# Normalising the residual: row sums with its formation, squares on ScalarE, scale and bias in one operation

## Time and profile before

| | before |
|---|---|
| median of 3 runs | 555.94 us (555.14 to 557.07) |
| the profiled execution | 554.49 us, its span 552.7 us |
| PE matmul busy | 446.5 us (81%) |
| DVE busy | 438.0 us (79%) |
| ACT busy | 376.4 us (68%) |
| POOL busy | 262.7 us (48%) |
| chain that ended last | PE 45%, DVE 25%, ACT 13%, issue 6%, DMA 6% |
| `stats` of `r` (L763), 32 instructions | 408 to 430 ns each |
| scaling of `r` (L664), 32 instructions | 583 to 601 ns each |
| L1168, 8 instructions | 1209 to 1231 ns each |

### The profile page before, as it was taken

One profiled execution on the slowest core, in us unless ns is written; L12 is line 12 of the kernel. 1 busy time (PEld: TensorE's weight loads), 2 busy tenths in 40 slices (PEclk: granted clock), 3 DMA queues, 4 the chain that ended last, 5 costly groups with the idle time before them and its releaser, 6 DMA issues.

```text
span 552.7 us, 11601 instructions
## 1 busy us (share of the span) xinstructions
PE 446.5 (81%) x2730; PEld 385.8 (70%) x2730; DVE 438.0 (79%) x1423; ACT 376.4 (68%) x928; POOL 262.7 (48%) x194
## 2 busy tenths in 40 slices
PE   0196899967999996587978999999999999999200
PEld 0045888856888885446867897999999999999200
DVE  6999795999898988775887776877777777777185
ACT  5992864455667565884656676777777777777266
POOL 0000359545467877375155534444354444445446
PEclk9998999999999996897989999999999999999755
DMA  6302830032223574398146465545454467645495
GB/s 153 154 1 71 336 127 1 0 133 78 100 92 133 175 231 159 122 337 280 40 109 144 82 121 139 82 79 79 71 85 79 78 110 157 119 78 68 85 376 228
DMA packets 48190, 70.34 MB, mean 127 GB/s; under 512 B 7680, under 2 KB 37248, under 8 KB 47744
## 3 DMA queue, kind: packets, MB, share of 16 engines
q1 hardware_dynamic: 34832, 51.82, 29.1%
q0 software_dynamic: 13296, 17.80, 19.3%
HBM read 37.90 MB, written 31.70 MB: 126 GB/s over the span
## 4 chain that ended last, share of the span: by engine, by line
PE 45%; DVE 25%; ACT 13%; issue 6%; DMA 6%; SPq 2%; POOL 2%; DVEq 1%; ACTq 0%; another core or an unknown queue 0%; POOLq 0%
PE psum L1518 15%; PE psum L1542 13%; PE psum L1528 4%; DMA y_rows<-yw,row_of 3%; PE psum L1438 3%; PE psum L1502 2%; ACT acc L735 2%; DVE ws L958 2%; DVE st L763 2%; PE psum L1396 2%; ACT dump L674 2%; PE psum L1458 2%; DVE o L1170 1%; ACT ws L611 1%; PE psum L1409 1%
## 5 line engine op out<-in xcount | busy, mean ns | idle before, releaser
L1343 POOL DMA_INDIRECT y_rows<-yw,row_of x71 | 110.6, 1558 | 140.3 <-SPq L405 74.7
L1518 PE MATMUL psum<-ws,z_hl 128*128 x426 | 119.3, 416 | 12.6 <-DVE ws L958 5.6
L1542 PE MATMUL psum<-ws,h_hl 128*128 x852 | 116.5, 286 | 0.6 <-DVE h_hl L1124 0.6
L1542 PEld LDWEIGHTS psum<-ws,h_hl 128*128 128x128 f32 x852 | 104.1, 189 | 0.8 <-issue 0.8
L1518 PEld LDWEIGHTS psum<-ws,z_hl 128*128 128x128 f32 x426 | 76.2, 192 | 28.0 <-issue 14.9
L1299 POOL DMA_INDIRECT z_rows<-zn,pos x64 | 70.4, 1099 | 26.2 <-issue 17.6
L656 ACT ACTIVATE hg<-hb 128x512 f32<-128x512 f32 x71 | 44.9, 632 | 31.7 <-DVE hb L1118 26.0
L1438 PE MATMUL psum<-yf,it 128*128 128x256 f32 x256 | 60.8, 394 | 2.6 <-DVE r L1144 2.6
L619 ACT ACTIVATE z_f<-psum,gb 128x128 f32<-128x128 f32 x142 | 57.1, 452 | 6.6 <-PE psum L1502 2.7
L1409 PE MATMUL psum<-pm,ft 128*128 128x256 f32 x256 | 58.2, 382 | 0.4 <-DVE tmp L944 0.4
L649 ACT CAST h_hl<-psum 128x512 fp32r<-128x512 f32 x71 | 41.5, 585 | 24.9 <-PE psum L1528 23.2
(11 more groups left out here) (223 smaller groups left out, 826.0 us busy)
## 6 DMA issues: line engine op xcount, KB each, us to landing
z_in<-z_rows SPq DMA_DIRECT2D x71, 129.5 KB
w_raw<-in_dram SPq DMA_DIRECT2D x16, 512.0 KB, 5.7
xs<-in_dram SPq DMA_DIRECT2D x8, 512.0 KB, 5.5
x_dram<-xs SPq DMA_DIRECT2D x8, 512.0 KB
y_rows<-zn SPq DMA_DIRECT2D x8, 512.0 KB, 3.3
yr<-y_rows SPq DMA_DIRECT2D x8, 512.0 KB, 7.4
out_dram<-acc SPq DMA_DIRECT2D x6, 512.0 KB, 2.7
b1r<-in_dram SPq DMA_DIRECT2D x8, 256.0 KB
```

Of the source, the lines that this page charges most:

```text
L1343: pool.indirect_dma_start(y_rows, bass.IndirectOffsetOnAxis(ap=row_of[:, t:t + 1], axis=0), yw[t % 6][:, :], None, compute_op=ALU.add).the ...
L1518: last = TE.matmul(ps_h[q], z_hl[q][:, a, k], w_at(e, c, k * F, F), start=n == 0, stop=n == 5)
L1542: last = TE.matmul(ps_y[q], h_hl[q][:, a, k], w_at(e, c, 1024 + k * H, H), start=n == 0, stop=n == 11)
```

## The change

- The two instructions that form `r` become four of 256 columns, each with its row sum (`accum_out`). `bn_stats` and `bn_aggr` of `r` go. One small operation makes the negative mean and signals `r_mean`.
- ScalarE, in place of normalising `r`, squares `r` with the mean as bias and sums the squares into `mv[2]`, signals `var2`, and takes the root with the scale 1/H.
- VectorE computes `(r - mean) * ln_w` in four instructions, after `scales_x1` and `find` and before `point` (in the last step before all of them).
- The reciprocal of the deviation moves behind `place`; L1168 goes; the four instructions that added `ln_b` now multiply by the reciprocal too.

```diff
@@ sigma (ScalarE)
-                                     scale=(1.0, 1.0 / H, 1.0, (1.0 + EPS) / H)[slot]).then_inc(sem(f"sd{slot}"), 1)
+                                     scale=(1.0, 1.0 / H, 1.0 / H, (1.0 + EPS) / H)[slot]).then_inc(sem(f"sd{slot}"), 1)
@@ step (ScalarE)
                 if cur.live:
+                    act.wait_ge(sem("r_mean"), cur.b + 1)
+                    for k in range(4):
+                        last = nc.scalar.activation(dump[:, k], r[:, k], ACT.Square, bias=mv[2][:, k, 0:1],
+                                                    accum_out=mv[2][:, k, 1:2])
+                    last.then_inc(sem("var2"), 1)
                     sigma(cur, 2)
-                    act.wait_ge(sem("st_r"), cur.b + 1)
-                    for k in range(4):
-                        last = nc.scalar.activation(r[:, k], r[:, k], ACT.Identity, bias=rs[:, 2, 4 + k:5 + k],
-                                                    scale=rs[:, 2, k:k + 1])
-                    last.then_inc(sem("r_norm"), 1)
@@ step (VectorE)
-                    V.tensor_tensor(r[:, 0:2], c, s_sb[:, :, :], ALU.add)
-                    V.tensor_tensor(r[:, 2:4], c, s_sb[:, :, :], ALU.subtract).then_inc(sem("r_ready"), 1)
+                    for k in range(4):
+                        last = V.scalar_tensor_tensor(r[:, k], c[:, k % 2], 1.0, s_sb[:, k % 2], ALU.mult,
+                                                      ALU.add if k < 2 else ALU.subtract, accum_out=st[:, 2, 0, k:k + 1])
+                    last.then_inc(sem("r_ready"), 1)
                     dve.wait_ge(sem("r_ready"), cur.b + 1)
-                    stats(lambda k: r[:, k], 2)
+                    V.tensor_scalar(mv[2][:, :, 0], st[:, 2, 0, 0:4], -1.0 / H, None, ALU.mult).then_inc(sem("r_mean"), 1)
                     if n < B:
                         if tail.live:
                             scales_x1(tail)
                         if last_tail.live:
                             find(last_tail)
-                    do(inverse(cur, 2))
-                    V.scalar_tensor_tensor(rs[:, 2, 4:8], mv[2][:, :, 0], -1.0, rs[:, 2, 0:4], ALU.mult,
-                                           ALU.mult).then_inc(sem("st_r"), 1)
+
+                    dve.wait_ge(sem("r_mean"), cur.b + 1)
+                    for k in range(4):
+                        last = V.scalar_tensor_tensor(o[:, k], r[:, k], mv[2][:, k, 0:1], lwb[:, 0], ALU.add, ALU.mult)
+                    last.then_inc(sem("r_mid"), 1)
                     if n < B:
                         if last_tail.live:
                             point(last_tail)
@@ step (VectorE), behind mult(nxt, 0) and place(last_tail)
-                    dve.wait_ge(sem("r_norm"), cur.b + 1)
-                    do(V.tensor_tensor(o[:, :, :], r[:, :, :], lwb[:, 0].unsqueeze(1).to_broadcast([P, 4, H]), ALU.mult))
+                    inverse(cur, 2).then_inc(sem("st_r"), 1)
+                    dve.wait_ge(sem("st_r"), cur.b + 1)
+                    dve.wait_ge(sem("r_mid"), cur.b + 1)
                     for k in range(4):
-                        last = V.scalar_tensor_tensor(o[:, k], o[:, k], 1.0, lwb[:, 1], ALU.mult, ALU.add,
+                        last = V.scalar_tensor_tensor(o[:, k], o[:, k], rs[:, 2, k:k + 1], lwb[:, 1], ALU.mult, ALU.add,
                                                       accum_out=st[:, 1, 0, k:k + 1])
                     last.then_inc(sem("o_ready"), 1)
```

## The result

| | before | after |
|---|---|---|
| median | 555.64 us (555.14 to 557.07, 4 runs) | 563.69 us (562.65 to 565.03, 4 runs) |
| the profiled execution, its span | 554.49, 552.7 us | 565.03, 563.2 us |
| granted TensorE clock, mean | 0.942 | 0.923 |
| walk, first to last `r` | 130.95 us | 137.80 us |
| last `r` to the first expert matmul | 24.98 us | 25.21 us |

The account below looks back on a forecast made before the run. The walk was taken as a ring of VectorE (`r` to `mask`) and TensorE (`mask` to next `r`); terms 0.87-1.13+0.54+0.57+1.23+0.57-0.44 = +2.2 us on 555.94 gave 558.1 us, range 554.0 to 561.5.

Parts of the forecast that it names:

- Its sum: Walk over eight sequences: changes priced sequence by sequence add up to +2.2 us, forecast 558.1 us, chance 0.4.
- Group: VectorE, ahead of `point` and `mask`: four new `scalar_tensor_tensor` take 1.62 us, bounds 1.4 to 1.9.
- forming of `r`: VectorE, start of each step: four 256-column instructions with sums replace two; `r_mean` is issued at r+1.51.
- the late root: Sequence 3: ScalarE's root for x1, ready only at r+2.28, holds VectorE's reciprocal; it starts 0.76 earlier, not 1.45.
- L954 alone held: Sequences 2 and 5: x1 product waits for GpSimd's add; 0.64 lost in 2, earlier statistics win only 0.10 in 5.
- a ring: Steady step: `r` to `mask` on VectorE, `mask` to the next `r` on TensorE; work behind `mask` is cheap.
- rival (c): Sequence 2: TensorE's wait for `mask` becomes some 3.3 us and its clock falls; +3.1, total 561.2 us; chance 0.1.
- the remark on sequence 1: Sequence 1: the longer TensorE wait for `r` could also lower the clock, but has slack behind it.
- Rival (b): Sequences 2 and 5: GpSimd's port use also holds `r_mean`, 0.3 later in each; sum +2.8, 558.8 us; chance 0.2.
- Rival (a): Sequence 0: the new group gets the port at once, -2.8 in place of +0.87; total 554.5 us; chance 0.2.
- Rival (d): Low-clock stretch at 211 us ends at another moment, or tile DMA waits swallow or add time; about 556; chance 0.1.
- Sequence 7: Last step, where the new group precedes the x1 reciprocal: `mask` side ends at 230.08 against 230.54, about -0.44.

Follow-up runs that it names:

- e4: Changed kernel with the mean of `r` made by ScalarE in place of VectorE's `tensor_scalar`: 558.42 us, ratio 1.0086 to the kernel before.
- e5: Kernel before, with two idle VectorE instructions ahead of `point` in sequence 2 alone: 556.42 us, ratio 1.0043.
- e13: Changed kernel with idle matmuls ahead of `rank` in sequences 2 and 5, third batch: 555.79 us, ratio 1.0054 to the kernel before.
- e1: Changed kernel with idle matmuls ahead of `rank` in sequences 2 and 5, first batch: 558.38 us, ratio 1.0079 to the kernel before.
- e9: Changed kernel run again without edit, second batch: 563.17 us, ratio 1.0095 to the kernel before.
- e11: Changed kernel run again without edit, third batch: 558.80 us, ratio 1.0095 to the kernel before.
- e12: Changed kernel with the group `(r - mean) * ln_w` moved behind `place` in sequence 2 alone: 558.20 us, ratio 1.0078 to the kernel before.
- e2: Changed kernel with the group `(r - mean) * ln_w` moved behind `place`, first batch: 551.63 us, ratio 0.9940 to the kernel before.
- e10: Changed kernel with the group `(r - mean) * ln_w` moved behind `place`, third batch: 552.55 us, ratio 0.9976 to the kernel before.
- e6: Changed kernel with the group moved behind `place` and the mean of `r` made by ScalarE: 556.58 us, ratio 0.9970 to the kernel before.
- e7: Changed kernel, group behind `place`, mean on ScalarE, and three idle matmuls ahead of the `rank` of sequence 6: 556.11 us, ratio 0.9979 to the kernel before.
- e8: Kernel before, with four idle matmuls ahead of the `rank` of sequence 6: 559.72 us, ratio 1.0026.

## Why the prediction was wrong

**Its sum.** Group, forming of `r`, mean and the late root came out within 0.04 us of their terms, and what they make together within 0.07: +0.57 in sequence 3, +0.88 in 0, -1.20 in 1. In sequences 2 and 5 the agreement is partly luck: with L954 alone held, as the sum had it, e4 shows +0.37 and +0.89 for `mask`, not +0.54 and +1.23, since `find` starts there at r+2.39 and r+2.99, where the sum had it at r+2.52 and r+3.30. `mult` of sequence 0 started at 104.24; less the 0.82 by which the walk began later that is 103.42, as predicted. The way from `r` to `mask` to the next `r` as a ring is shown.

**The step that failed** is rival (c). The prediction had the mechanism, in sequence 2, at +3.1 with a chance of 0.1, because the new wait of 3.3 us lies "between" 2.73 without a fall and 4.29 with one; the sum was made without it. In every profile of the changed kernel the wait was 3.37 and the clock fell, which cost 2.51 us in the sixteen matmuls and 0.22 in the short ones. A value between two ends, one harmless and one costly, is no reason for a chance of 0.1. The price of the fall was near: +3.1 put, 2.7 measured in sequence 2. The second place, sequence 5, was not looked at: there the wait grew from 1.15 to 2.02 and the fwd cost 1.68 more, though 2.73 in the earlier trace rows had kept its speed; the sum has no term for the clock there and the rivals none either. Only the remark on sequence 1, a fall with slack behind it, came true as written. e5 and e13 show the step in sequence 2 from both sides: lateness alone brings the 2.6 us, and filled waits take them away with `mask` as late as in the changed kernel. In sequence 5 only the filled wait was tried.

**Rival (b)** happened too, and its price was right: 0.3 in each of sequences 2 and 5, where e4 against the changed kernel shows 0.28 and 0.37. Against the sum it shows as 0.11 and 0.03 only, because the sum's own terms for the held L954 were 0.17 and 0.34 too large. And (b) and (c) are no alternatives, since one feeds the wait of the other. Put together afterwards, the terms with (c) in both places give 555.94+2.2+0.1+4.4 = 562.6; the prediction, which let only one of them be true at a time and (c) in one place, had 561.2 as its worst rival.

**Rival (a)** did not come in the changed kernel: all six profiles with the group early in sequence 0 and the mean on VectorE (after, e1, e9, e11, e12, e13) have the mean held over the last addition, for 4.48 to 4.52 us. **Rival (d)** did not come there either: the sixteen matmuls of sequence 6 took 6.67, 6.63 and 6.70, as before. But it is a thing that happens, as e5, e12 and e13 show, and it is worth 1.3 to 1.9 us.

**Sequence 6 and the rest.** +0.09 in place of +0.57: TensorE is indeed 0.60 later at the inverse, but ScalarE, which sets this step, had no pause of 0.42 before its copy this time. Sequence 7 has `mask` at r+5.23 in place of 5.74, -0.51 as the step had it, but `r` to the first expert matmul grew by 0.23. Of the 8.05 us, 6.85 are the walk of the profiled execution; with e9 and e11 at 5.4 and 5.0, some 2.5 to 3 us of the first result look like scatter between sets of runs. On the two later chips the forecast's +2.2 and the clock's 3.0 (e13 against e11) make up the whole, and e13 itself lies 2.0 above the kernel before. That this is so near +2.2 is partly luck, since e13's profile has the shorter stretch in sequence 6, and its walk is 1.12 longer than the one before and not 2.65. Why the first four runs lay higher is not settled.

## What to carry to other kernels

When an edit lengthens a wait of TensorE, price the wait twice: its own length, and the work behind it at half the clock; a wait that kept its speed once is no proof for another of that length, so a fall belongs in the sum, not in a rival with a small chance. Look for it at every repeat of the pattern, and let rivals add up where one feeds the other. And put new VectorE work behind the signal that others wait for: the change with its group ahead of `mask` costs 5 us or more, and with the same group behind it gains 1 to 2.5.

## What the runs showed of the hardware

- TensorE stood at the lower of its two levels (granted 0.50, 1.2 GHz) behind waits of 3.37 and 3.52 us, and kept its speed behind 2.73 and 3.10; yet it took 5.39 us for the next sixteen matmuls behind 2.02, and 5.15 behind 2.23. In sequence 5 the same place shows both outcomes: 3.70 for the sixteen behind 1.97 (e2), 1.95 (e10) and 1.69 (e6), and 5.39 behind 1.69 (e7) and behind 2.01 or 2.02 (after, e9, e11, e12). The length of a wait alone does not tell whether the clock falls; what decides was not found. The Trainium skill (TensorE: Matmul & The Clock Gate, Part 1) says that how many matmuls run slow at a kernel's start varies from run to run of the same kernel. The two groups of times of e4 would agree, but three profiles of the changed kernel (after, e9, e11) fell in the same places and for 6.20, 6.10 and 6.24 us.
- A `tensor_scalar` of four elements stood for 4.51 us beside GpSimd's additions, over three boundaries between them; in e2 it came in after 0.79 us, at the first, and in e10, the same program, after 4.48.
- ScalarE stood 5 to 9 us before L603 in three kernels (e6, e7, e8), on something that the trace does not name.
- The walk begins between 95.3 and 98.5 us from execution to execution. In the three profiles that begin at 98.4 to 98.5 (e1, e8, e12) the granted clock was 0.50 from 71 to 74 us, and in the other eleven it was 1.00 there.
- Single times of one kernel spread mostly over 3 to 7 us; one execution of e2 took 631.78 us, at a mean granted clock of 0.736.
